# Recurrent step of a fused GNN and LSTM kernel: tanh of the gates into the cell's PSUM bank, and a second wait in front of it

## The reference, cut to what matters

```
i_t = sigmoid(xi_t + h @ V_i);  g_t = tanh(xg_t + h @ V_c);  o_t = sigmoid(xo_t + h @ V_o)
c_new = h * c + i_t * g_t
h_new = o_t * tanh(c_new)
```

## Time and profile before

| | us |
|---|---|
| median of the three runs | 17562.97 |
| lowest and highest | 17558.74 and 17570.36 |
| span of the profiled execution | 17545.4 |
| median less span | 17.6 |
| of the span, the recurrent loop | 9355 |

### The profile page before, as it was taken

One profiled execution on the slowest core, in us unless ns is written; L12 is line 12 of the kernel. 1 busy time (PEld: TensorE's weight loads), 2 busy tenths in 40 slices (PEclk: granted clock), 3 DMA queues, 4 the chain that ended last, 5 costly groups with the idle time before them and its releaser, 6 DMA issues. The chain is left out here.

```text
span 17545.4 us, 683245 instructions
## 1 busy us (share of the span) xinstructions
PE 12730.7 (73%) x250869; PEld 10213.3 (58%) x250870; DVE 11697.3 (67%) x68713; ACT 5986.8 (34%) x41949; POOL 5631.1 (32%) x6174
## 2 busy tenths in 40 slices
PE   5247773399655656556888888888888888888887
PEld 3135552266444544445777777777777777777776
DVE  7368887322555454556777777777777777777777
ACT  0004442011100101003555555554555555555555
POOL 4778887666576575772000000000000000000000
PEclk6558886599877777775555555555555555555555
DMA  0102222111333333331000000000000000000000
GB/s 22 25 21 73 74 72 43 56 34 33 101 105 98 96 105 87 105 105 37 4 4 4 4 4 4 4 4 4 4 4 4 4 4 4 4 4 4 4 4 18
DMA packets 352412, 609.44 MB, mean 35 GB/s; under 512 B 157501, under 2 KB 232222, under 8 KB 348988
## 3 DMA queue, kind: packets, MB, share of 16 engines
q0 software_dynamic: 223104, 471.33, 10.4%
q1 hardware_dynamic: 126524, 100.27, 1.9%
HBM read 508.72 MB, written 62.45 MB: 33 GB/s over the span
## 5 line engine op out<-in xcount | busy, mean ns | idle before, releaser
L2402 PE MATMUL lr_ZI<-ls_h,ls_V 128*128 128x1 f16 x150000 | 5006.8, 166 | 1669.7 <-DVE ls_h L2451 1412.8
L2402 PEld LDWEIGHTS lr_ZI<-ls_h,ls_V 128*128 128x128 f16 x150000 | 4487.3, 104 | 2677.0 <-DVE ls_h L2451 2640.4
L2419 ACT ACTIVATE ls_tg<-lr_ZI 128x2 f32<-128x2 f32 x12500 | 2150.0, 172 | 4626.5 <-PE lr_ZI L2402 4534.6
L2446 DVE TENSOR_TENSOR_SCAN lr_c<-ls_tg,ls_one_hc 128x2 f32<-128x2 f32 x12500 | 2118.1, 170 | 1441.0 <-ACT ls_tg L2419 1317.8
L2358 POOL COPY ls_HT<-ls_h 128x250 f32 x50 | 19.8, 395 | 9358.3 <-DVE ls_h L2456 9358.3
L2402 PE MATMUL lr_ZO<-ls_h,ls_V 128*128 128x1 f16 x75000 | 2865.0, 165 | 0.0
L671 PE MATMUL prop_sum<-prop_G,prop_S 128*128 128x256 f32 x4992 | 1830.4, 546 | 1369.9 <-DMA prop_G<-hop_table,prop_idx 1369.9
L657 POOL DMA_INDIRECT prop_G<-hop_table,prop_idx x2496 | 2368.3, 949 | 1057.3 <-issue 708.8
L2402 PEld LDWEIGHTS lr_ZO<-ls_h,ls_V 128*128 128x128 f16 x75000 | 2483.2, 104 | 0.0
L671 PEld LDWEIGHTS prop_sum<-prop_G,prop_S 128*128 128x128 f32 x4992 | 1403.9, 288 | 1796.3 <-issue 1486.1
L2451 DVE TENSOR_TENSOR ls_h<-ls_to 128x1 f16<-128x1 f32 x12500 | 2023.4, 162 | 479.1 <-ACT ls_to L2424 16.0
(11 more groups left out here) (455 smaller groups left out, 13965.7 us busy)
## 6 DMA issues: line engine op xcount, KB each, us to landing
prop_G<-hop_table,prop_idx POOLq DMA_INDIRECT x2496, 2.7
mow_W<-in_L_ffn_W SPq DMA_DIRECT2D x16, 1024.0 KB, 10.8
moe_out<-me_Ys SPq DMA_DIRECT2D x108, 128.0 KB, 1.7
all_X<-gat_table,gs_idx POOLq DMA_INDIRECT x832, 2.8
hop_table<-ht_T SPq DMA_DIRECT2D x50, 256.0 KB, 2.1
sd_records<-sc_rec,sc_place POOLq DMA_INDIRECT x784
ss_records<-me_recs,me_places POOLq DMA_INDIRECT x540
gat_table<-gt_hs SPq DMA_DIRECT2D x50, 128.0 KB, 1.8
```

The costliest lines, as they stand in the source:

```text
L2402: mm = nc.tensor.matmul(place(hf, bank, col, 1), (V2 if part == "21" else V1)[:, q, ROWS.index(row), :], hx[:, prev, q, 1:2], start=False, ...
L2419: nc.scalar.activation(tg[:, s % 2, m, :], place(hf, m, col, 2), ACT.Tanh, scale=back).then_inc(gates[m], 1)
L2446: nc.vector.tensor_tensor_scan(c[m][:, 0:2], tg[:, e, m, :], one_hc[:, m, :], 1.0, ALU.mult, ALU.add).then_inc(cell[m], 1)
```

## The change

ACT writes tanh of the gates of block m to columns 2 and 3 of the cell's own PSUM bank `c[m]`, in place of `tg` in SBUF, which goes. The scan reads them there. As ACT now writes to a bank that DVE reads and writes, it waits before each of the two tanh for h times c of the same block, DVE's last access to that bank in the step before. That needs one semaphore for each block. The wait for the gates (`z[m]`) is written first, the one for `hc_made[m]` second. The scan of block 0 waits for block 1's `hc_made`. The arithmetic stays.

```diff
-        tg = ph.sb("tg", [P, 2, KD, 2])
...
-            h_made, hc_made, kept = (pr.sem(n) for n in ("h", "hc", "kept"))
+            hc_made = [pr.sem(f"hc{j}") for j in range(KD)]
+            h_made, kept = pr.sem("h"), pr.sem("kept")
+            CELL, GATED = slice(0, 2), slice(2, 4)
...
                                 act.wait_ge(z[m], t + 1)
-                                nc.scalar.activation(tg[:, s % 2, m, :], place(hf, m, col, 2), ACT.Tanh, scale=back).then_inc(gates[m], 1)
+                                act.wait_ge(hc_made[m], t + 1)
+                                nc.scalar.activation(c[m][:, GATED], place(hf, m, col, 2), ACT.Tanh, scale=back).then_inc(gates[m], 1)
...
-                    nc.vector.memset(one_hc[:, :, 1], 0.0).then_inc(hc_made, 1)
+                    for m in range(KD):
+                        nc.vector.memset(one_hc[:, m, 1:2], 0.0).then_inc(hc_made[m], 1)
...
                                 if m == 0:
-                                    dve.wait_ge(hc_made, t + 1)
-
-                                nc.vector.tensor_tensor_scan(c[m][:, 0:2], tg[:, e, m, :], one_hc[:, m, :], 1.0, ALU.mult, ALU.add).then_inc(cell[m], 1)
+                                    dve.wait_ge(hc_made[KD - 1], t + 1)
+                                nc.vector.tensor_tensor_scan(c[m][:, CELL], c[m][:, GATED], one_hc[:, m, :], 1.0, ALU.mult, ALU.add).then_inc(cell[m], 1)
...
-                            nc.vector.tensor_tensor(one_hc[:, 0, 1:2], h[:, r, 0:1], c[0][:, 1:2], ALU.mult)
-                            nc.vector.tensor_tensor(one_hc[:, 1, 1:2], h[:, r, 1:2], c[1][:, 1:2], ALU.mult).then_inc(hc_made, 1)
+                            for m in range(KD):
+                                nc.vector.tensor_tensor(one_hc[:, m, 1:2], h[:, r, m:m + 1], c[m][:, 1:2], ALU.mult).then_inc(hc_made[m], 1)
```

## The result

The changed kernel takes 17620.51 us (median of 6 runs, 17618.23 to 17624.48), the kernel before in the same comparison 17560.37 us (17555.98 to 17570.36). The ratio is 1.0034, 95% interval 1.0023 to 1.0045: slower by 60 us. That lies in the range that was forecast (17535 to 17700), but it isn't the forecast itself (17571, no change that can be measured). It is near what the prediction called the middle values of rival A (70 us), of which, though, as will be seen, only a part came by A's way.

The account below looks back on a forecast made before the run. The prediction took the recurrent step's latency as the bound, a ring of engine waits with sigmoid 0 pinning the tanh of cell 0. Regular steps 6250 x 0 plus 8 us for irregular ones, on 17563, gave 17571 us; range 17535 to 17700.

Parts of the forecast that it names:

- rival A: Before the gates' tanh, the wait for hc decides: 21 ns a step, 131 us, 17702; middle values 70 us; chance 0.22.
- The bound of the step: Recurrent loop: latency of engines' mutual waits; tanh of cell 0 follows sigmoid 0, not scan 0; regular step stays 1.48 us.
- R = 0.10: ACT, end of hc to start of the gates' tanh: the wait written second stands alone, taking 0.10 us, bounds 0.03 to 0.11.
- s = 0: DVE's scan reading the gates from PSUM: no extra time, taken as 0 within -3 to +4 ns.
- The estimate of 65 ns more: DVE's PSUM access by the skill's fixed cycles, 120 against 58: 65 ns more, which the prediction's rows did not show.
- a block's second cell tanh moves up to 0.07 behind its sigmoid: ACT, block 1: the cell's tanh starts 20 ns earlier, 0.07 behind sigmoid 1, and hc follows earlier too.
- a late h costs more: Irregular steps with DVE's h late: scan 0 comes 80 ns later in about 100 steps, 8 us.
- half of a lateness is given back: Regular step: a positive lateness lengthens it by about half, as later products leave hc more room in the next step.
- L: Lateness in ns at block 0 from the wait for hc: 475 - min(g,20) + R - 540 - g + s - 7.
- The gain g: ACT's gates' tanh writing PSUM instead of SBUF: 20 ns shorter on 172, bounds 0 and 44.
- The slack of block 0: Gates of block 0, ahead of the tanh of cell 0: 7 ns of delay is free, rounding allows 0 to 10.
- behind ACT's waiting instruction only ACT's own work queues: ACT at the wait for hc: what queues behind needs the gates first anyway; no cost counted.

Follow-up runs that it names:

- run 6: Changed kernel with h times c made earlier, by one instruction per block from sigmoid, tanh and cell: 17533.52 us, ratio 0.9991 to the kernel before.
- run 2: Changed kernel with the wait for h times c written first and the gates' wait second: 19950.39 us, ratio 1.0182 to the kernel before.
- run 1: Changed kernel with the gates back in SBUF in two buffers, ACT's wait for h times c kept: 19724.01 us, ratio 1.0069 to the kernel before.
- run 8: Changed kernel with one spare DVE product ahead of the two that make h times c: 17820.74 us, ratio 1.0156 to the kernel before.
- run 3: Kernel before plus a second, early-satisfied wait (on h1 of the step before) ahead of each gates' tanh: 19592.19 us, ratio 1.0003.

## Why the prediction was half right

**What held.** The bound of the step (sigmoid 0, the chain of waits): run 6. The order of the waits, with R = 0.10: measured 0.099, and run 2. The scan from PSUM, s = 0: 170 ns before and after. The estimate of 65 ns more, worked out from the fixed cycles in the Trainium skill, "VectorE: DVE Perf Modes", section on the TRN2 errata, is not borne out for this instruction. That a block's second cell tanh moves up to 0.07 behind its sigmoid. That a late h costs more, though the 8 us agree by luck: forecast were about 100 steps at 80 ns, measured are 45 with 98 ns more each (4.4 us), and gaps at `hc` 0, which the prediction didn't count, add 3.6. And that half of a lateness is given back: runs 1 and 8.

**The step that failed first: L was put at -12 ns and is above zero, about +3.** Two of its terms were mis-sized.
- The gain g of the PSUM target was taken as 20 and is 15 (172 to 157). It stands in the formula twice, as the shorter tanh and as the earlier `hc` through block 1, so 5 ns too much are 10 in L. The Trainium skill, "ScalarE: Activation LUTs", section "Step-by-step: what each stage is for", says that ScalarE reaches PSUM faster than SBUF. The trace agrees: 157 against 172 ns.
- The slack of block 0 was taken as 7 ns, from 0.04 against 0.03. In ns the edge from scan 0 to the tanh is 39.6 where sigmoid 0 pins it and 33.1 where it doesn't (run 8). But the tanh itself lasts 166 ns in the first case and 171 in the second, so its end has a slack of (39.6 + 166) - (33.1 + 171) = 1.5 ns. The slack of a start is not that of an end.

With these, L = 475 - 15 + 99.5 - 540 - 15 - 1.5 = 3, so 1.5 ns a step; measured are 2.9. Along the path in the records, the weight load of the 30th product, and sigmoid 0 with it, comes 1.3 ns later after PE's start than before (773.0 and 771.7), and the tanh of cell 0 is 1.4 longer (167.6 and 166.2). The first is itself not explained. The 475 and 540 were read from rows with two places; the records put `hc` 0 62.4 ns ahead of the tanh and not 65, and with that L is 5.6 and its half 2.8. So how much of the 2.9 is the wait's, between 1.5 and nearly all, the formula can't tell. In sum 18 us where 0 were forecast.

**The step that was missing: 28.8 us.** The prediction said that behind ACT's waiting instruction only ACT's own work queues, which needs the gates anyway. That is true of the work, but the next instruction can also reach the engine late. By my reading the lone wait holds everything behind it until `hc` has come, 99 ns before the tanh starts, and in that time ACT can't make up for a gap of about 0.28 us in its stream of instructions, which before was spent while it waited for the gates. The clearest case is in the table: 0 such steps before, 45 with the tanh of gates 0 late by 0.28. The evidence is the record of the wait, which comes on time with the tanh 349 ns behind it, and runs 1, 2, 3 and 6: the gaps are there where the lone wait ends last (run 1: 45 steps, 12 us; run 2: the same 45), and with a wait that is over early none of the 45 is left (5.7 and 5.9 us in all). The Trainium skill, "Perfetto Trace Analysis", section "Per-engine timelines", describes for ACT and DVE a queue in which an instruction waits for its semaphores while the sequencer goes on to the next. This fits, if a wait that stands alone keeps the sequencer from going on. The traces show the effect, not the queue, nor why the instructions come late every 142 steps. The prediction knew of the same gaps on DVE and did not ask why ACT showed none.

**The sum**: 18 us for the regular steps, 28.8 for ACT's gaps, 8 for late h and `hc`, 7.3 for DVE's other events (their gaps now meet a step without slack; argued, not shown, as nothing that was tried takes them apart), less 1.0 for steps with nothing late in the list: 61 us, the difference of the two loops. Of rival A's way (`hc` decides in a regular step) it is the first term alone; that its middle value of 70 us fits the whole is in part chance.

What stays open: the 1.3 ns of PE, what makes the gaps on ACT, and why the 5 ns of its ninth product come in some kernels and steps only. Whether a change of the order of ACT's instructions could move sigmoid 0, and so make the 15 ns count, was not tried.

## What to carry to other kernels

In a loop that is bound by its latency, a second wait in front of an instruction has two prices: the longer way from signal to start (here 0.10 in place of 0.03 us), and that it seems to hold what is behind it, so that gaps in the engine's stream of instructions, until then hidden, are added. It cost nothing that could be measured where what it waits for was early by more than both (runs 3 and 6); so first make the signal early, or write the waits so that the one that ends last, the longer way of the other counted in, rides on the instruction. A shorter instruction gains nothing while another engine's signal pins its successor, and a slack of a few ns has to be taken from the end of the next instruction, in ns, before a term of 5 ns that counts twice is set against it.

## What the runs showed of the hardware

- Tanh of two elements for each partition, from PSUM: 172 ns into SBUF, 157 into PSUM. A scan of two elements takes 170 ns whether its first input is in SBUF or PSUM.
- From the end of the producer to the start of the consumer: 33 ns where the wait rides on the instruction, 99 on ACT where it stands alone ahead. The profile names the producer that signalled last, and so put only 99 of the cases down to `hc`, which decided in 90% of the steps.
- ACT starts an instruction 67.5 ns after the one before it, for the first pair after a pause; and the same tanh is 166 ns long when it starts so and 171 when it starts on a signal.
- Gaps of about 0.28 us ahead of an instruction that waits for nothing: on ACT, at the tanh of gates 0, 45 times, mostly 142 steps apart and at the same steps in the changed kernel and in runs 1 and 2. With the signal early (runs 3 and 6) they cost nothing.
- A product of three single elements by `scalar_tensor_tensor` takes 208 ns, where `tensor_tensor` with two takes 149 to 155.
